# Alternating the bank of the attention's weighted sums, and respreading the first tiles, the weights' maxima and the experts' turning

## What is computed

```python
xn = layernorm(x)                      # x: [8, 1024, 128]
K, V = xn @ proj_k, xn @ proj_v        # one key and value head for all
Q = einsum('bnd,hdk->bhnk', xn, proj_q)
W = softmax(einsum('bhnk,bmk->bhnm', Q, K), axis=-1)
Y = einsum('bhnv,hdv->bnd', einsum('bhnm,bmv->bhnv', W, V), proj_o)
F = einsum('aemn,enh->amh', einsum('amh,ehn->aemn', xn, w1), w2)   # 8 experts, no nonlinearity
out = x + Y + F
```

## Time and profile before

| | us |
|---|---|
| median of 3 runs (1715.01, 1715.02, 1720.04) | 1715.02 |
| profiled execution, its own time | 1721.89 |
| its span, first to last instruction | 1720.1 |
| TensorE matmul busy | 1664.0 (97%) |
| GpSimd / ScalarE / VectorE busy | 1334.9 / 1293.4 / 1280.9 |

### The profile page before, as it was taken

One profiled execution on the slowest core, in us unless ns is written; L12 is line 12 of the kernel. 1 busy time (PEld: TensorE's weight loads), 2 busy tenths in 40 slices (PEclk: granted clock), 3 DMA queues, 4 the chain that ended last, 5 costly groups with the idle time before them and its releaser, 6 DMA issues. The chain is left out here.

```text
span 1720.1 us, 46064 instructions
## 1 busy us (share of the span) xinstructions
PE 1664.0 (97%) x18808; PEld 1220.2 (71%) x18808; DVE 1280.9 (74%) x2754; ACT 1293.4 (75%) x1294; POOL 1334.9 (78%) x955
## 2 busy tenths in 40 slices
PE   6689999999999999999999999999999999999997
PEld 5567777777777777777777777777777777777774
DVE  4467777777777777777777777777777777777774
ACT  3467777777777777777777777777777777777774
POOL 0377887887887887888878878878878878788786
PEclk8899999999999999999999999999999999999999
DMA  7000000000000000000000000000000000000000
GB/s 223 1 2 2 2 2 8 8 2 2 2 13 3 2 2 2 14 2 2 2 8 8 2 2 2 8 8 2 2 2 8 8 2 2 2 14 2 2 2 13
DMA packets 16142, 16.70 MB, mean 10 GB/s; under 512 B 384, under 2 KB 12160, under 8 KB 15936
## 3 DMA queue, kind: packets, MB, share of 16 engines
q1 hardware_dynamic: 13856, 12.72, 2.5%
q10 hardware_dynamic: 2080, 1.05, 0.2%
HBM read 9.57 MB, written 4.19 MB: 8 GB/s over the span
## 5 line engine op out<-in xcount | busy, mean ns | idle before, releaser
L252 POOL TENSOR_TENSOR pr_lo<-pr,pr_hi 128x1024 f16<-128x1024 f32 x512 | 1087.6, 2135 | 338.8 <-ACT pr_hi L333 331.7
L326 ACT ACTIVATE pr<-s_ps,boost,scale 128x1024 f32<-128x1024 f32 x512 | 617.0, 1205 | 258.9 <-PE s_ps L457 240.9
L634 DVE TENSOR_REDUCE key_max<-s_ps 128x128 f16<-128x1024 f32 x512 | 625.9, 1223 | 0.5
L333 ACT ACTIVATE pr_hi<-pr 128x1024 f16<-128x1024 f32 x512 | 525.4, 1051 | 8.1
L455 PE MATMUL s_ps<-g_lo,xT 128*128 128x128 f16 x4096 | 516.1, 220 | 2.2 <-DVE g_lo L647 0.9
L457 PE MATMUL s_ps<-g_hi,xT 128*128 128x128 f16 x4096 | 515.6, 220 | 0.0
L455 PEld LDWEIGHTS s_ps<-g_lo,xT 128*128 128x128 f16 x4096 | 401.0, 98 | 42.3 <-DVE g_lo L647 10.1
L457 PEld LDWEIGHTS s_ps<-g_hi,xT 128*128 128x128 f16 x4096 | 402.5, 98 | 30.4 <-issue 0.6
L363 PE MATMUL t_ps<-pr_hi,xn_hi 128*128 128x512 f16 x1024 | 389.3, 380 | 21.0 <-POOL pr_lo L252 7.3
L365 PE MATMUL t_ps<-pr_hi,xn_lo 128*128 128x512 f16 x1024 | 389.2, 380 | 0.0
L364 PE MATMUL t_ps<-pr_lo,xn_hi 128*128 128x512 f16 x1024 | 389.2, 380 | 0.0
(11 more groups left out here) (108 smaller groups left out, 1548.8 us busy)
## 6 DMA issues: line engine op xcount, KB each, us to landing
out_dram<-xacc SPq DMA_DIRECT2D x16, 256.0 KB, 2.3
w_sb<-in_L_ffn_w_dram SPq DMA_DIRECT2D x1, 2048.0 KB, 12.9
xacc<-in_L_attn_x_dram SPq DMA_DIRECT2D x1, 640.0 KB, 7.9
pr<-in_L_attn_proj_q_dram ACTq DMA_DIRECT2D x1, 512.0 KB, 4.6
pr<-in_L_attn_proj_o_dram ACTq DMA_DIRECT2D x1, 512.0 KB, 6.8
wkv<-in_L_attn_proj_k_dram SPq DMA_DIRECT2D x1, 64.0 KB, 2.8
wkv<-in_L_attn_proj_v_dram SPq DMA_DIRECT2D x1, 64.0 KB, 4.4
w_sb<-in_L_ffn_w_dram SPq DMA_DIRECT2D x1, 0.5 KB, 19.1
```

Source lines behind the costliest of these rows:

```text
L252: pool.tensor_tensor(pr_lo[:, u % RING, :], pr32[:, u % PR, :], pr_hi[:, u % RING, :], ALU.subtract)\
L326: act.activation(pr32[:, u % PR, :], both_banks(u), ACT.Exp, bias=boost[:, 0:1], scale=scale[:, 0:1])\
L333: act.activation(pr_hi[:, u % RING, :], pr32[:, u % PR, :], ACT.Copy).then_inc(p_hi_ready, 1)
L634: dve.tensor_reduce(key_max[:, u % 2, :], both_banks(u).rearrange("p (t q) -> p q t", q=P), AX_X, ALU.max).then_inc(keys_max, 1)
```

## The change

There is no `turn_ps` any more: `t_ps` has two banks, the sum of block k goes to bank k % 2, and the maxima are turned in the other one (for n % 4 = 2 the first turn goes to a bank of the scores). Tiles are spread two to a period; tile 0 of a block moves from the period n % 4 = 3 to the end of the period before it, its first matmul ahead of `turn_keys_max`, and takes its wait for `p_lo_ready` along. `place_bias` is always first. The weights' maxima are spread by two small matmuls and a VectorE reduction, not by GpSimd. The first tiles are normalised in groups of 4, 4 and 2; five experts are turned inside the loop. GpSimd's power moves to n % 8 = 4 and `xn_lo` to n % 8 = 5; the last `p_low` and the last addition move to VectorE. The core of the diff:

```diff
+    FIRST_TILES = ((0, HT), (HT, HT), (NT, AHEAD - NT))
-        t_ps = pb("t_ps", [P, BANK])
-        turn_ps = pb("turn_ps", [P, BANK])
+        t_ps = pb("t_ps", [P, 2 * BANK])
+        def sum_bank(k):
+            return t_ps[:, (k % 2) * BANK:(k % 2 + 1) * BANK]
 ...
-            sp.dma_start(xacc[:, 0:AHEAD, :], x_tiles[:, 0:AHEAD, :]).then_inc(x_in, 16)
+            sp.dma_start(xacc[:, 0:HT, :], x_tiles[:, 0:HT, :]).then_inc(x_in[0], 16)
+            sp.dma_start(xacc[:, HT:NT, :], x_tiles[:, HT:NT, :]).then_inc(x_in[1], 16)
+            sp.dma_start(wo_sb, wo.rearrange("h d v -> d h v")).then_inc(o_in, 16)
+            sp.dma_start(xacc[:, NT:AHEAD, :], x_tiles[:, NT:AHEAD, :]).then_inc(x_in[2], 16)
 ...
# gpsimd
-            spread_max(0)
+            xn_low(HT, HT, HT)
-                if n == 2:
-                    spread_max(1)
-                if n == 8:
-                    spread_max(2)
-                if n % 8 == 7 and (tile := ln_tile(n // 8)) is not None:
+                if n % 8 == 4 and (tile := ln_tile(n // 8)) is not None:
+                    pool.wait_ge(ln_var, tile - AHEAD + len(FIRST_TILES) + 1)
                     pool.tensor_tensor(rstd[:, AHEAD:AHEAD + 1], var_eps[:, AHEAD:AHEAD + 1],
                                        minus_half[:, 0:1], ALU.pow).then_inc(ln_rstd, 1)
-                if n % 8 == 4 and (tile := ln_tile(n // 8 - 1)) is not None:
+                if n % 8 == 5 and (tile := ln_tile(n // 8 - 1)) is not None:
+                    xn_low(tile, 0, 1)
-                if 1 <= n <= UNITS:
+                if 1 <= n < UNITS:
                     p_low(n - 1)
# tensor
+            def row_of_amax(weight, n):
+                pe.wait_ge(amax_ready, weight + 1)
+                pe.matmul(amax_row(n), amax[:, weight:weight + 1], ident[:, :], start=True, stop=True)
+            def spread_amax(weight, n):
+                pe.wait_ge(amax_found, weight + 1)
+                pe.matmul(amax_spread_ps(n), ones_row[0:1, :], amax_one[0:1, weight:weight + 1], start=True, stop=True)
 ...
             def high_pass(u, half):
+                    if j == 3:
+                        pe.wait_ge(max_found, u)
 ...
+            def weigh(k, t, first, rest):
+                if first:
+                    if t == 0:
+                        pe.wait_ge(p_lo_ready, 4 * k + 4)
+                        if k >= 2:
+                            pe.wait_ge(t_lo_ready, k - 1)
+                        pe.wait_ge(bias_ready, min(4 * k + 6, UNITS))
+                        if k == 1:
+                            pe.wait_ge(f_copied, 1)
+                    pe.matmul(dst, xn_hi[:, tile, :], p_hi, start=t == 0, stop=False)
+                if rest:
+                    pe.matmul(dst, xn_hi[:, tile, :], p_lo, start=False, stop=False)
+                    done = pe.matmul(dst, xn_lo[:, tile, :], p_hi, start=False, stop=t == NT - 1)
 ...
+            def chunk(n, place, first=True, rest=True):
+                k, t = summing(n), 2 * ((n + 1) % 4) + 1 + place
+                if t == NT:
+                    k, t = k + 1, 0
+                if k == -2 and rest:
+                    turn_w1(t)
 ...
             for n in range(PERIODS):
+                at = n % 4
                 if n < UNITS:
                     high_pass(n, 0)
-                if 1 <= n <= UNITS and not row_later:
+                if 1 <= n <= UNITS and at != 3:
                     max_to_row(n - 1)
                 if n < UNITS:
                     high_pass(n, 1)
+                if 1 <= n <= UNITS and at == 3:
+                    max_to_row(n - 1)
                 chunk(n, 0)
-                if 1 <= n <= UNITS and row_later:
-                    max_to_row(n - 1)
-                chunk(n, 1)
                 small_products(n)
                 if 1 <= n <= UNITS:
                     low_passes(n - 1)
+                if at == 2:
+                    chunk(n, 1, rest=False)
                 if n < UNITS:
                     turn_keys_max(n)
-                chunk(n, 2)
+                chunk(n, 1, first=at != 2)
# vector
-                if 1 <= n <= UNITS and not row_later:
+                if 1 <= n <= UNITS:
                     place_bias(n - 1)
                 if n < UNITS:
                     max_of_keys(n)
-                if 1 <= n <= UNITS and row_later:
-                    place_bias(n - 1)
 ...
# before_bias: bn_stats of a later tile at n % 8 = 2 -> 0, its mean 3 -> 1, var_eps 6 -> 3,
# normalise (L577) at n % 8 = 2 of the next pair -> 7, split_high (L583) 3 -> 4; c_lo at n = 5 -> 8
+                if n == UNITS + 1:
+                    p_low_last()
+            dve.tensor_tensor(xacc[:, last:last + 2, :], xacc[:, last:last + 2, :], y_tmp[:, 1, :, :], ALU.add)\
+               .then_inc(y_added, 1)
```

More of the change, by code:

```diff
@@ L184, in turn_tile @@
             pair, at = divmod(n, 8)
-            return pair + NT if at == 0 and pair + NT < TILES else None
+            if n == 4:
+                return NT
+            return pair + NT if at == 0 and pair >= 1 and pair + NT < TILES else None
         def ln_tile(pair):
@@ L236, in _, with xn_low @@
             pool.memset(centre[0:1, 0:1], 0.0).then_inc(consts, 1)
[L238 to L245, removed]
-            spread_max(0)
+            for g, (first, count) in enumerate(FIRST_TILES):
+                pool.wait_ge(ln_var, g + 1)
+                pool.tensor_tensor(rstd[:, first:first + count], var_eps[:, first:first + count],
+                                   minus_half[:, 0:count], ALU.pow).then_inc(ln_rstd, count)
+            def xn_low(tile, row, tiles):
+                pool.wait_ge(ln_hi, tile + tiles)
+                pool.wait_ge(xn_ready, tile)
+                at = tile % KEEP
+                pool.tensor_tensor(xn_lo[:, at:at + tiles, 1:D], xn32[:, row:row + tiles, 1:D],
+                                   xn_hi[:, at:at + tiles, 1:D], ALU.subtract).then_inc(xn_ready, tiles)
+            xn_low(HT, HT, HT)
             def p_low(u):
@@ L389, in _, with turn_tiles @@
             last.then_inc(folded, 1)
[L391 to L394, removed]
+            def turn_tiles(first):
+                pe.wait_ge(xn_ready, first + HT)
+                if first:
+                    pe.wait_ge(xT_ready, first)
+                for t in range(first, first + HT):
+                    at = (t - first) * 2 * P
+                    pe.transpose(turn16[:, at:at + P], xn_hi[:, t, :], ident16[:, :])
+                    last = pe.transpose(turn16[:, at + P:at + 2 * P], xn_lo[:, t, :], ident16[:, :])
+                last.then_inc(xT_ps, 1)
@@ L398, in _ @@
                 last.then_inc(w1_turned, 1)
[L400 to L408, removed]
@@ L497, in fold_ffn @@
                     last.then_inc(f_ps, 1)
-            def chunk(n, place):
-                k, tiles = weighed(n)
-                for t in tiles[place]:
-                    if k == -1:
-                        fold_ffn(t)
-                    if 0 <= k < BLOCKS:
-                        weigh(k, t)
+            def chunk(n, place, first=True, rest=True):
[4 more added lines that the diff above has]
+                    turn_w1(t)
+                if k == -1 and rest:
+                    fold_ffn(t)
+                if 0 <= k < BLOCKS:
+                    weigh(k, t, first, rest)
             def head_out(k, g):
@@ new lines, in normalise_first @@
+            def normalise_first(g):
+                first, count = FIRST_TILES[g]
+                dve.wait_ge(ln_rstd, first + count)
+                for t in range(first, first + count):
+                    normalise(t, t, t)
+            tile_stats(0)
+            tile_stats(1)
+            normalise_first(0)
+            tile_stats(2)
+            normalise_first(1)
+            dve.wait_ge(ln_hi, HT)
+            dve.tensor_tensor(xn_lo[:, 0:HT, 1:D], xn32[:, 0:HT, 1:D], xn_hi[:, 0:HT, 1:D], ALU.subtract)\
+               .then_inc(xn_ready, HT)
@@ L717, in before_bias @@
                     normalise(tile, AHEAD, 0)
-                if at == 3 and (tile := ln_tile(pair - 1)) is not None:
-                    split_high(tile, 1, tile + 1)
+                if at == 4 and (tile := ln_tile(pair - 1)) is not None:
+                    split_high(tile, 0, 1)
+                if n == 0:
+                    normalise_first(2)
+                if n == 1:
+                    split_high(NT, NT, AHEAD - NT)
                 if n == 1:
```

260 lines of the change are left out of this document (164 added, 96 removed).

## The result

The changed kernel takes 1752.09 us (1751.85 to 1755.65), the kernel before 1717.53 in the same series: ratio of the runs 1.0205, 95% interval 1.0179 to 1.0231. It is 2% slower; 1688 was forecast. The profiled execution has a span of 1749.8 us, 29.7 more than before.

A forecast was written before the change was run, and what follows sets the result against it. TensorE was taken to bound the kernel, with waits for VectorE's read and the row of maxima. Start -28, earlier wait +5, late pairs -2, end -2 sum to -27: from the 1715.0 median 1688 us, range 1660 to 1708.

The forecast's parts named there:

- Two banks: Tile 0 no longer waits for `t_low`, 0.27 us less a block; with the `place_bias` wait gone too, pairs 25.64 to 24.90.
- The earlier wait for the low parts: Tile 0's first matmul waits for GpSimd's low parts one period earlier, 0.84 us; pairs 25.74 against 25.64, +5 us in all.
- E: Moment when the low passes of a period n % 4 = 2 are out and the turn of the maxima starts.
- late pairs: Last ten pairs, no layernorm left: wait 0.32 us every second block, 25.28 against 25.50 a pair, -2 us.
- VectorE's order: In n % 4 = 2, `high_pass`'s new wait for `max_found` is hidden by 0.04 us; uncovered, at most 0.1 a block.
- Rival C: `split_high` on VectorE, moved to n % 8 = 4, misses its gap between GpSimd low parts: +39 us, 1722; chance 0.07.
- The start: Before and early in the loop: GpSimd's three maximum spreadings go; second read of a sum at 78.2, -28 us.
- 9.5 of waits: Waits in us added up to n = 14: experts through one bank, VectorE's a_lo, a weight's maximum and c_lo, first units.
- The end: After the loop: the last low part on VectorE beside GpSimd's last but one; -2 us, between -3 and -0.5.

## Why the prediction was wrong

**Two banks: right.** Without both waits a pair was to take 24.90; with GpSimd's and the port's waits out of the way it takes 24.91.

**The earlier wait for the low parts: right to 0.02 us.** Forecast were 25.74 a pair; the six undisturbed pairs take 25.73. Ready at E + 13.32 against 12.48 was 0.84 of waiting; the longest waits are 0.8. In the late pairs 25.28 was forecast, and the steps are 12.49 and 12.80, 25.29. The two kernels with the power moved and the one with tile 0 moved confirm the chain from three sides.

**VectorE's order: this step failed.** It looked at waits between TensorE and VectorE only, allowed at most 0.1 a block, and had no price for where normalise lands; 1.17 a pair was lost there. The earlier trace rows had the means: a cast that takes 197 or 542 ns, according to whether GpSimd is busy. Rival C carried this over to the one operation, `split_high`, whose row showed it, and gave it 0.07. For that operation C was right: asked for 0.20 us into the addition, as C had laid it, the cast won its gap in the changed kernel. Normalise takes 327 to 346 ns everywhere in the old trace, so that nothing there tells that it can be held; but it always ran while GpSimd was idle (812.31, between 811.38 and 813.79), so its row could not tell. Both ends should have been set for it: 0.33, and 0.33 plus a whole low part, 2.13. In the kernel before, `find_max` of n % 8 = 7 ends 1.48 us after GpSimd's first low part starts (802.58 against 801.10), in the changed one 2.09 (810.99 against 808.91). So a look at the trace of before would have put normalise beside a low part; whether it then wins the gap hangs on less than 0.2 us, which those rows could not give, so both ends were open. Its price is 1.17 us a pair, not the 1.97 of the delay. The wait of tile 0 absorbs nothing of it (0.83 here, 0.84 with normalise moved away). With normalise moved away, VectorE itself waits 0.4 longer for TensorE before `place_bias`, and the row of maxima is ready 0.8 before the low passes take it; with normalise in front both reserves are used up, the low passes start 0.75 late, and the next turn and high passes, which wait for VectorE too, lose 0.4 more. 46 x 1.17 = 54 us of the miss of 64.

**The start: right in its cause, 6 us too good.** -22 in place of -28. The term that was mis-sized is the one that I "cost at nothing": the loads. I watched those of the first tiles and of wo; the statistics of tile 10 were moved ahead to where they wait for the last load, 7.03 us. Between the two kernels that differ in this alone it is worth 7.9 at the second read (85.7 to 77.8); without it the forecast of 78.2 is met, though its 9.5 of waits is a sum of terms that, as listed, make 9.3. One part alone, the spreading, gives -27. That the loop begins 4.2 earlier than with the spreading alone leaves only 1.4 at the second read (77.8 against 79.2); what takes the rest no run shows.

**The end: -3.4, not -2** (steps 11.67, 10.49 and 6.83 in place of 11.93, 9.72 and 10.93, and 6.0 behind the last in place of 6.6, less the three removed waits of 0.27). The Trainium skill ("SBUF — State Buffer", section "Who interferes with whom") says that a VectorE instruction with two SBUF inputs contends with a GpSimd instruction that reads SBUF, and that the one issued second is blocked until the other is done. The trace agrees, in both directions: VectorE's low part ends 1.08 after GpSimd's last one (1737.04 against 1735.96), and the addition asked for meanwhile ends 0.60 after VectorE's (1737.64).

**The sum** with what was measured: -22 + 5 + 54 - 2 - 3 = +32, against 34.6 by the medians. **The range** was wrong in its upper end: C was a case of one operation with 0.07, though five operations of VectorE had been moved against GpSimd's. For two of them, normalise and `split_high`, the runs show that they can be held; the other three (statistics, mean and var_eps) take what they took before, 0.28, 0.17 and 0.14.

## What to carry over

Where an operation of one engine can hold one of another, moving an operation can move it into the other's shadow: lay every moved operation over the other engine's rows, and price it at a whole operation of the other engine if the trace has no case of both at once. A resource freed (a bank) pays only when the next wait in line is looked up first; here it was GpSimd's chain, and each 0.5 us taken off that chain paid 0.5 us until the block next door became late. Before work is pulled forward, look up what load it stands behind.

## What the runs showed of the hardware

**A short operation can be held though its row never told.** Normalise, a VectorE operation of 127 columns with two scalars from SBUF, takes 0.33 us alone, longer than a cast of as many columns (0.197). Beside a GpSimd low part it is held up to 1.97 us. The statistics, one input of 128 columns, are not: in the changed kernel 52 of them are asked for beside a low part, seven of these 0.1 or 0.2 us into it, and all take 0.28 or 0.29. Here is one (its low part runs to 815.90):

```profile
815.51 0.28 DVE L843 BATCH_NORM_STATS2 stats<-xacc 128x6 f32<-128x128 f32 x1
...
813.77 2.13 POOL L297 TENSOR_TENSOR pr_lo<-pr,pr_hi 128x1024 f16<-128x1024 f32 x1
```

**When the gap closes.** Whatever the moment at which one of the two operations that can be held, normalise and the cast of `split_high`, was asked for in the first 1.9 us of a low part of 2.13, it ended 2.21 to 2.23 after that low part's start, also with the next one ready behind it. For normalise these moments were 0.32, 0.92, 1.19, 1.38, 1.82 and 1.88 us (it took 1.90, 1.30, 1.03, 0.84, 0.40 and 0.35), for the cast 0.24 (1.98) and, in the kernel before, 1.68 (0.54). Asked for at 1.99 to 2.02, normalise lost 46 times of 52, took 2.30 and ended at 4.30: that is the same 2.21 behind the start of the next low part, for rows of successive GpSimd operations start 2.09 apart. It won 6 times, all at 1.99 or 2.00, with 0.34, where the two low parts together took 4.32 or 4.33 in place of 4.22. So the gap closes between 1.88 and 2.01 us, before the row of the low part has ended. That GpSimd's next operation has by then taken its place in line is my reading; no run shows the line itself, nor what it is that the two engines share.
